# Moving the low parts of split weights from VectorE to GpSimd in the first stage of a two-stage transformer kernel, with a new timetable for the splitting

## What is computed

```python
x = x + layernorm(mqa(layernorm(x)))        # first stage: 16 query heads of width 8, one K and one V head, causal
x = x + layernorm(layers(layernorm(x)))     # second stage: 6 layers
# one of the 6 layers:
#   qkv = shift(x) @ Wqkv[i]        128 x 3072: 16 heads of 64; q and k l2-normalised, scaled, rotated
#   local attention, windows of 32, keys of the window before and of the own window; @ Wo[i]; + x
#   layernorm, @ W1[i] (128 x 682), a * gelu(gate), @ W2[i]; + x
```

## Time and profile before

| what | value |
|---|---|
| median of 3 runs | 3322.84 us |
| the profiled execution | 3326.02 us, of it 3324.3 us from the first to the last instruction, mean granted clock 0.987 |
| first stage | 0 to about 430 us; steady part from about 40 to 390 us |
| PE busy in the whole span | 96% |
| GpSimd busy in the whole span | 89% |
| TensorE clock | full in the steady part but for a short stretch at 385 us; half of it from 402 us to 436 us |

### The profile page before, as it was taken

One profiled execution on the slowest core, in us unless ns is written; L12 is line 12 of the kernel. 1 busy time (PEld: TensorE's weight loads), 2 busy tenths in 40 slices (PEclk: granted clock), 3 DMA queues, 4 the chain that ended last, 5 costly groups with the idle time before them and its releaser, 6 DMA issues.

```text
span 3324.3 us, 158297 instructions
## 1 busy us (share of the span) xinstructions
PE 3192.2 (96%) x64569; PEld 2745.6 (83%) x64570; DVE 2753.2 (83%) x5217; ACT 2758.3 (83%) x4558; POOL 2951.2 (89%) x3529
## 2 busy tenths in 40 slices
PE   6999868999999999999999999999999999999997
PEld 5666547888888888888888888888888888888886
DVE  7777667888888888888888888888888888888886
ACT  4777647888988888988888988888888888888885
POOL 6688567999999999999999999999999999999996
PEclk9999879999999999999999999999999999999999
DMA  2222112432334232333232333232342232332322
GB/s 82 85 82 67 44 47 67 119 73 67 81 82 115 73 73 67 81 85 114 72 74 67 87 78 114 72 74 71 84 123 68 71 75 71 85 96 69 76 64 77
DMA packets 179955, 263.67 MB, mean 79 GB/s; under 512 B 44296, under 2 KB 67280, under 8 KB 179664
## 3 DMA queue, kind: packets, MB, share of 16 engines
q1 hardware_dynamic: 179792, 261.98, 30.4%
HBM read 43.54 MB, written 16.78 MB: 18 GB/s over the span
## 4 chain that ended last, share of the span: by engine, by line
PE 77%; issue 4%; DVE 3%; ACT 2%; POOL 2%; POOLq 0%; DVEq 0%; ACTq 0%
PE ring L1515 11%; PE ring L1474 10%; PE ring L1524 9%; PE proj L1465 8%; PE score L1493 7%; PE proj L1466 7%; PE proj L1467 7%; PE ring L1500 4%; PE ring L1577 3%; PE ring L1568 2%; PE ring L1569 2%; PE ring L1570 2%; PE ring L1546 1%; PE ring L1552 1%; DVE sumsb L1748 1%
## 5 line engine op out<-in xcount | busy, mean ns | idle before, releaser
L1372 POOL TENSOR_TENSOR by_cos<-by_cos,by_sin 128x1024 f32<-128x1024 f32 x384 | 917.1, 2388 | 16.0 <-DVE by_sin L1744 15.8
L1378 POOL TENSOR_TENSOR by_cos<-by_cos,norms 128x1024 f32<-128x1024 f32 x384 | 731.1, 1904 | 21.2
L1742 DVE TENSOR_TENSOR by_cos<-proj,turns 128x512 f32<-128x512 f32 x768 | 522.0, 680 | 195.7 <-PE ring L1474 109.7
L1465 PE MATMUL proj<-qkv_hi,xs_hib 128*128 128x512 f32 x1152 | 533.8, 463 | 27.1 <-ACT vb L1612 11.2
L1744 DVE TENSOR_TENSOR by_sin<-proj,turns 128x512 f32<-128x512 f32 x768 | 523.0, 681 | 0.0
L1748 DVE TENSOR_REDUCE sumsb<-squares 128x16 f32<-128x1024 f32 x384 | 464.5, 1210 | 0.0
L1633 ACT ACTIVATE squares<-proj 128x512 f32<-128x512 f32 x768 | 444.2, 592 | 22.6 <-PE proj L1467 9.7
L1466 PE MATMUL proj<-qkv_lo,xs_hib 128*128 128x512 f32 x1152 | 458.2, 398 | 0.0
L1467 PE MATMUL proj<-qkv_hi,xs_lob 128*128 128x512 f32 x1152 | 457.6, 397 | 0.0
L1474 PE MATMUL ring<-ident,by_cos 128*128 128x128 f32 x3072 | 411.9, 277 | 1.2 <-issue 1.2
L1515 PEld LDWEIGHTS ring<-pTb,v_win 64*64 64x64 f32 x24576 | 380.3, 135 | 35.9 <-issue 27.2
(11 more groups left out here) (189 smaller groups left out, 7369.4 us busy)
## 6 DMA issues: line engine op xcount, KB each, us to landing
v_win<-vb SPq DMA_DIRECT2D x1152, 128.0 KB, 2.4
v_win<-vb SPq DMA_DIRECT2D x768, 64.0 KB, 2.0
in_qkv<-L_ffn_Wqkv SPq DMA_DIRECT2D x36, 256.0 KB, 3.2
qkv_low<-qkv_lo SPq DMA_DIRECT2D x30, 256.0 KB, 2.1
in_qkv<-L_ffn_Wqkv SPq DMA_DIRECT2D x10, 768.0 KB, 5.9
in_lo<-qkv_low SPq DMA_DIRECT2D x10, 768.0 KB, 7.6
wo<-L_ffn_Wo SPq DMA_DIRECT2D x12, 256.0 KB, 3.9
turns_kept<-turns SPq DMA_DIRECT2D x5, 512.0 KB, 2.7
```

Of the source, the lines that this page charges most:

```text
L1372: nc.gpsimd.tensor_tensor(both, both, by_sin[:, j, :], ALU.add).then_inc(e[f"{w_}_added"].sem, 1)
L1378: nc.gpsimd.tensor_tensor(heads, heads, inverse, ALU.mult).then_inc(e[f"{w_}_ready"].sem, 1)
L1465: nc.tensor.matmul(out, xs_hi[:, tile], qkv_hi[:, cols], start=True, stop=False)
L1742: nc.vector.tensor_tensor(of_heads(by_cos[:, t % 2, j, cols]), heads, table(0), ALU.mult)
```

## The change

Three tables take the place of two. HIGH_AT has the steps of the high parts, LOW_AT those of the low parts. In each batch there are now 5 pieces (h = 2, 6, 7, 10, 14), and one more at h = 15 in batches 0 and 1. The six pieces of layer 0 come at steps 129, 130, 137, 138, 141 and 142. The low part follows 4 steps after the high part, or 3, so that it falls on h = 2, 6, 10 (two pieces) and 14. For the 41 pieces whose low part lies in a step under 128 it is computed by GpSimd, right behind `causal` of that step; the other 7 stay on DVE. SP stores one step after the low part. The four rotation tables of GpSimd move from h = 5, 6, 12, 13 to h = 2, 6, 10, 14, behind the low parts, and SP stores them at h = 15 instead of 14.

```diff
-SPLIT_AT = [MQA_H * b + h for b in range(B) for h in (1, 5, 7, 9, 13, 15)]
-TURN_AT = (5, 6, 12, 13)
+HIGH_AT = sorted([MQA_H * b + h for b in range(B) for h in (2, 6, 7, 10, 14)] + [15, 31]) + [129, 130, 137, 138, 141, 142]
+LOW_AT = [n + (3 if n % 4 == 3 else 4) if n < HEADS else n + {129: 4, 130: 4, 137: 2, 138: 2, 141: 5, 142: 15}[n] for n in HIGH_AT]
+TURN_AT = (2, 6, 10, 14)
@@ SP
-                for i, at in enumerate(SPLIT_AT):
-                    if n == at - 4:
+                for i in range(len(SPLITS)):
+                    if n == LOW_AT[i] + 1 and SPLITS[i][:2] != ("qkv", 0):
+                        store_split(i)
+                    if n == HIGH_AT[i] - 4:
                         load_split(i)
-                    if n == at + 2 and SPLITS[i][:2] != ("qkv", 0):
-                        store_split(i)
...
-                if batch_of(b) and b < DEPTH - 1 and h == 14:
+                if batch_of(b) and b < DEPTH - 1 and h == 15:
                     store_turns(DEPTH - 1 - b)
@@ GpSimd
+            def split_low(i):
+                cols = piece_of(i)[-1]
+                pool.wait_ge(split_hi, i + 1)
+                nc.gpsimd.tensor_tensor(ready["lo"][:, cols], ready["in"][:, cols], ready["hi"][:, cols].bitcast(F32),
+                                        ALU.subtract).then_inc(split_lo, 1)
...
                 if 0 <= n < HEADS:
                     causal(n)
+                for i in range(len(SPLITS)):
+                    if n == LOW_AT[i] and n < HEADS:
+                        split_low(i)
                 if batch_of(b) and b < DEPTH and h in TURN_AT:
                     rotation_table(DEPTH - 1 - b, TURN_AT.index(h))
@@ ScalarE
-                if n in SPLIT_AT:
-                    split_high(SPLIT_AT.index(n))
+                if n in HIGH_AT:
+                    split_high(HIGH_AT.index(n))
@@ VectorE
-                if n - 1 in SPLIT_AT:
-                    split_low(SPLIT_AT.index(n - 1))
+                for i in range(len(SPLITS)):
+                    if n == LOW_AT[i] and n >= HEADS:
+                        split_low(i)
```

## The result

Four runs each on one chip: the changed kernel 3354.18 us median (3352.41 to 3355.41), the kernel before 3324.03 (3320.92 to 3325.38). The ratio is 1.0086 with a 95% interval of 1.0073 to 1.0099: **slower by 0.9%**, inside the range forecast and 8 us above the 3346 forecast. The profiled execution took 3352.41 us with a span of 3350.7, 26.4 more than the span before.

The account below looks back on a forecast made before the run. PE was taken as fullest but not the only bound, since it waits for GpSimd's L368. Batches +19.1, DVE -0.7, stage end +0.7, clock +4.5 gave +23.6 us: 3346.4 against 3322.84, range 3330 to 3362.

Parts of the forecast that it names:

- end of the stage: Steps from 126 on, with layer 0's pieces: narrow low part, late load of step 134; +0.7 us, bounds -1 and +3.
- h = 2 to 6, 6 to 10, 10 to 14, 14 to 2: Four segments of a middle batch between PE's transposes, lengthened by low parts and tables on GpSimd: together +3.3 us.
- batches 0 to 7, without the clock: First stage: the segments' added time over all eight batches, +19.1 us in sum.
- DVE's waits: PE's waits for DVE's maxima, 7.4 us; DVE, lighter by 0.69 us per piece, gives 0.7 back.
- clock: TensorE at half clock after new long waits in the first stage: 0 to +15 us, three stretches taken, +4.5.
- Contention: A low part on DVE slows a `causal` beside it; leaving gives GpSimd 0.19 us per segment, 0.45 more in the second.
- A sign that failed: PE's waits for L368, the maxima's second column, should grow from 14.0 to 25 us or more.
- The second stage should keep its length: Sign named for the second stage: no change in its length.
- my main case: GpSimd's chain as worked out, few clock falls: 3346 us, own range 3336 to 3353, chance 0.63.
- the rival in which the clock falls behind every long wait: Half clock after all of about ten long PE waits: 15 us instead of 4.5, 3357 us; chance 0.20.
- GpSimd has room: Rival: GpSimd's 7.85 us idle per batch takes the low parts and waits vanish, 3310 us; chance 0.10.
- the loop starts with L368 itself: Argument against the room rival: work between two L368 delays the second almost one for one; the loop's 1.33 us stays idle.

Follow-up runs that it names:

- The experiment without the subtraction: Kernel before, with each low part's subtraction on VectorE replaced by a memset of zeros: 3321.17 us, ratio 0.9988.
- The memset experiments: Low parts on VectorE, 41 one-column memsets on GpSimd: 3331.25 us; 7 more: 3331.4; changed kernel plus 7 memsets: 3349.69.
- the memset kernel: Changed kernel with low parts on VectorE and 41 one-column memsets on GpSimd in their place: 3331.25 us, ratio 1.0016 against the kernel before.

## Why the prediction came out as it did

In the first stage the mechanism and the terms held, and the total was 1.5 us too high; the second, which I had said would keep its length, came out 4.3 us longer. Some of the closeness is luck: one fall of the clock more than I took (1.5 us) and one that I had overlooked (1.5 us the other way) cancel, and the end of the stage, forecast +0.7 and measured +0.5, moves by more than that from profile to profile.

| step | forecast | measured |
|---|---|---|
| h = 2 to 6, 6 to 10, 10 to 14, 14 to 2 | +1.05, +0.12, +1.3, +0.85 | +1.07, +0.10, +1.38 without the clock's 1.5, +0.85 |
| batches 0 to 7, without the clock | 1.8, 1.1, 4.6, 3.3, 3.3, 3.6, 0.7, 0.65 | 1.7, 0.7, 4.6, 3.4, 3.4, 3.6, 0.3, -0.6 |
| DVE's waits | -0.7 | from 7.4 to 7.0 us; inside the row above |
| clock | +4.5, three stretches | +6.0, four stretches, less 1.5 for the one at 385 us, now gone |
| end of the stage | +0.7 | +0.5 |
| first stage | 23.6 | 22.1 |
| second stage | 0 | +4.3 |

- *Price on GpSimd.* 1.24 us from start to start, as L321's row gave it. The recorded mean is 1.29: the Trainium skill's advice (Perfetto Trace Analysis, GPSIMD Engine Instruction) to take distances between starts agrees with the 2.49 us for two.
- *Contention.* `causal` is back at 0.41, so 0.19 a segment is right by this row. The experiment without the subtraction gives 0.11 to 0.18 a segment and 0.44 for the second, a bit under my 0.19 and 0.64. Full exclusion for the whole instruction, as the Trainium skill has it (SBUF — State Buffer, SBUF: two separate sides), would have given 0.34 by my estimate; no run here shows that much.
- *A term that was left out.* A fall of the clock in the kernel before, 1.5 us at 385 us in batch 7, was in my rows and not in my sum. It went with the change, and in every experiment too.
- *A sign that failed.* PE's waits for the maxima's second column grew to 16.6 us and not to 25 or more. The third segment's wait went to 0, and in its place stands the new wait for `causal`, 17.5 us in all; I should have named the sum of the two. The waits for `causal`, 1.84 and 1.08 us in batch 4, are each about 0.25 longer than forecast, with the segments as forecast.
- *The clock.* Of the six waits of 1.81 to 2.34 us for `causal` at h = 13, four were followed by half clock at 1.5 us each (those of batches 1 and 5 were not). Batch 1, without a fall, gives the check: its third segment grew by 1.26, that of batch 2, with one, by 2.82. A fifth fall, at 148 us in batch 2 behind a wait of 1.68, cost nothing, since GpSimd was late there anyway; the waits of 1.08 and 1.35 brought none. Three was an estimate with bounds of none and all. Why four of these six waits were followed by a fall and two not stays open.
- *The step that failed: "The second stage should keep its length".* GpSimd's stop of 4.35 us in the last layer makes PE 4.7 us later. VectorE's stops moved as well. The one before the change, 3.45 us at floors (first row below), is followed by a wait of PE for VectorE (second row), and with both gone PE gains 2.8. Behind the one of 2.92 us at probs in the changed kernel, which ends at 3005.29, PE falls back 1.9. Together that makes +3.9. The rest is -2.7 by 543 us, where the clock ramps up, +2.7 spread over 2400 us, and +0.4 at the end. The memset experiments show GpSimd's stop to go with the number of instructions ahead of it. The slow +2.7 appears with more instructions (+1.7 in the memset kernel) but also, at +2.1, in one without them; it stays open, as do the 1 to 4 us by which any two profiles here differ between 438 and 543 us. The two rows (timelines of DVE and PE, kernel before):

```profile
2960.92 0.22 DVE L1753 TENSOR_REDUCE floors<-sumsb 128x32 f32<-128x64 f32 x1 [3.45 <-issue]
2963.59 1.54 PE L1577 MATMUL ring<-hidden,w 128*128 128x256 f32 x6 [2.44 <-DVE hidden L1831]
```

- *The medians* differ by 30.2, the spans by 26.4. The profiled run of before was 2.0 above its median and that of the changed kernel, the lowest of its four, 1.8 below.
- *The rivals.* By its time alone the result, 3354.18, lies 1 us above my main case's own range (3336 to 3353) and 3 us below the rival in which the clock falls behind every long wait (3357). The rows decide: four falls that cost 1.5 us, not ten. "GpSimd has room" was wrong for this place of the low parts and nearly right for another: behind L369 the same work fits, first stage -7.9. My argument that "the loop starts with L368 itself" holds for work behind the second `causal` half. I had counted the 1.33 us as closed to any work, where it is closed only to work that is issued behind the wait.

## What to carry to other kernels

An engine that runs its list in order can use the time in which one of its instructions waits only for work that stands *ahead* of that instruction in the list. One position later the same work costs time, less what it fills of later waits: here a part of 1.24 us cost 1.07 in the segment without such a wait and 0.10 in the one with 0.48 us of it, VectorE's relief included in both. Before moving work to an engine with idle time, find each idle piece's row, place the work directly ahead of the instruction named there, and check that each segment stays below the next engine's need. Here two pieces at one step cost more than two at two steps, on either engine.

## What the runs showed of the hardware

- A GpSimd stop of 2.1 to 4.4 us marked "issue" goes with the place in the engine's instruction stream: with 41 more instructions, of whatever work, it falls on by_cos of the last layer (4.35, 3.7, 4.34, 3.8 us), with 48 on newton_b (2.62, 2.40, 2.05), and with none more no such row is seen. VectorE has a like one, 3.5 us at floors before, 2.9 at probs with 41 instructions fewer, and ScalarE one of 2.1 us at vb of the last layer in every run. A packet of 8 KB of a queue marked "instruction" lands in those looked at (GpSimd's seven, VectorE's and ScalarE's before and with the change), 1.2 to 1.5 us before the end.
- In the changed kernel the granted clock fell to half, 1.2 GHz, behind five of PE's seven waits of 1.68 to 2.34 us for `causal`; a wait of 2.7 us at 68 us had no fall right behind it. In the kernel before it fell behind one of 1.3 us. With the low parts on GpSimd at the old steps it fell at four of the ten waits of 1.69 to 3.93 us for L369's counterpart. So the length of a wait alone doesn't tell. A fall cost 1.5 us of sixteen value products, and taking the wait from 1.84 to 0.56 removed it.
- An engine's busy sum says little of what it costs: 43.55 and 43.62 us of GpSimd work made batches of 45.76 and 51.55 us.
